# Perceiver of four layers on one core: identity products of TensorE taken out at nine places

## The reference, cut to what matters

```python
x = x + L0_xattn(ctx, ctx, _layernorm(x), ...)
x = x + L0_attn(_layernorm(x), ...)       # gated linear attention
x = x + L0_ffn(_layernorm(x), ...)        # 8 routed experts and 1 shared
x = x + L1_xattn(_layernorm(x), ctx, mask, ...)
x = x + L1_attn(_layernorm(x), ...)
x = x + L1_ffn(_layernorm(x), ...)        # 4 experts
x = x + L2_xattn(_layernorm(x), ctx, bias, ...)   # with a norm, a feed forward and a norm of its own
x = x + L2_attn(_layernorm(x), ...)
x = x + L2_ffn(_layernorm(x), ...)        # 4 rounds over 4 experts
x = x + L3_xattn(_layernorm(x), ctx, ctx, ...)
x = x + L3_attn(_layernorm(x), ...)
x = x + L3_ffn(_layernorm(x), ...)        # low rank

def _layernorm(x, axis=-1, eps=1e-05):
    m = jnp.mean(x, axis=axis, keepdims=True)
    v = jnp.var(x, axis=axis, keepdims=True)
    return (x - m) / jnp.sqrt(v + eps)
```

## The kernel before

| place | line | call | behind | ahead of | at us |
|---|---|---|---|---|---|
| 1 | L735 | (2, 2) | projection of the L0 cross attention | norm, L0 attention | 41.3 |
| 2 | L779 | (2, 2) | projection of the L0 attention | norm, gates and feed forward L0 | 80.4 |
| 3 | L791 | (2, 2) | feed forward L0 | norm, L1 cross attention | 186.8 |
| 4a, 4b | L1070 | (2, 1) | projection in `self_attention`, called for L1 and L3 | norm, feed forward L1 / L3 | 436.0, 1151.3 |
| 5 | L1176 | (2, 2) | feed forward L1 | norm, L2 cross attention | 481.1 |
| 6 | L1319 | (2, 1) | projection of the L2 cross attention | norm, its feed forward | 623.9 |
| 7 | L1322 | (2, 9) | its feed forward | two norms in a row, L2 attention | 646.2 |
| 8 | L1370 | (2, 2) | feed forward L2, four rounds | norm, L3 cross attention | 990.0 |
| 9 | L1378 | (2, 1) | projection of the L3 cross attention | norm, L3 attention | 1113.0 |

## Time and profile before

### The profile page before, as it was taken

The page is one execution under the profiler, slowest core; times in us unless marked ns, Lnnn a source line. Parts: engine busy times, 40 slices in busy tenths (PEclk is TensorE's granted clock), DMA queues, the critical chain, the costliest instruction groups (busy, mean ns, idle before and its releaser), DMA issues.

```text
span 1173.2 us, 26800 instructions
## 1 busy us (share of the span) xinstructions
PE 1087.7 (93%) x9262; PEld 752.1 (64%) x9262; DVE 678.1 (58%) x2030; ACT 581.1 (50%) x1288; POOL 347.3 (30%) x550
## 2 busy tenths in 40 slices
PE   7879998999999789899998878899999999999987
PEld 4455665787777556566665456677777776666554
DVE  5575445545555573678784775534343434788774
ACT  5542224343333464577774352634343444678665
POOL 2216101211121213355541141221304040466560
PEclk9989999999999998999999979999999999999989
DMA  8700130222232001355642412011111111100000
GB/s 264 261 1 21 33 85 8 62 48 57 57 56 62 1 2 34 122 167 160 164 132 87 102 32 47 14 54 52 57 41 55 53 55 45 50 2 2 1 2 20
DMA packets 69307, 75.32 MB, mean 64 GB/s; under 512 B 12048, under 2 KB 61472, under 8 KB 68840
## 3 DMA queue, kind: packets, MB, share of 16 engines
q1 hardware_dynamic: 67032, 66.50, 20.5%
q0 software_dynamic: 1376, 7.49, 2.0%
q10 hardware_dynamic: 816, 0.20, 0.1%
HBM read 71.55 MB, written 2.10 MB: 63 GB/s over the span
## 4 chain that ended last, share of the span: by engine, by line
PE 79%; DVE 8%; ACT 5%; DMA 3%; issue 2%; POOL 2%; ACTq 1%; SPq 0%; DVEq 0%; POOLq 0%
PE PS L566 13%; PE PS L578 12%; PE PS L1205 7%; PE PS L1216 6%; PE PS L853 5%; PE PS L817 5%; PE PS L569 3%; PE PS L860 2%; PE PS L1237 2%; PE PS L804 2%; PE PS L1194 2%; ACT XN L1446 2%; PE PS L1187 1%; PE PS L843 1%; PE PS L1232 1%
## 5 line engine op out<-in xcount | busy, mean ns | idle before, releaser
L578 PEld LDWEIGHTS PS<-WB,AR 128*128 128x128 f32 x1504 | 181.6, 192 | 42.7 <-issue 38.8
L578 PE MATMUL PS<-WB,AR 128*128 128x128 f32 x1504 | 182.3, 275 | 0.6 <-DVE X L2084 0.5
L1446 ACT ACTIVATE AR<-PS,WB 128x512 f32<-128x512 f32 x160 | 109.9, 687 | 144.7 <-PE PS L566 136.9
L2084 DVE SCALAR_TENSOR_TENSOR ACC<-PS,SM,ACC 128x128 f32<-128x128 f32 x192 | 54.1, 344 | 95.8 <-PE PS L578 94.8
L1959 DVE TENSOR_TENSOR AR<-PS,AR 128x512 f32<-128x512 f32 (+2 forms) x71 | 49.8, 701 | 92.8 <-issue 38.6
L566 PE MATMUL PS<-ZT,WB 128*128 128x512 f32 x208 | 101.1, 609 | 0.7 <-DMA WB<-in_units 0.7
L1205 PE MATMUL PS<-AR 64*128 64x257 f32 x512 | 90.6, 429 | 1.0 <-POOL AR L2929 1.0
L1446 ACT ACTIVATE AR<-PS 128x512 f32<-128x512 f32 (+2 forms) x83 | 43.8, 528 | 85.5 <-PE PS L569 69.1
L566 PE MATMUL PS<-XNT,WB 128*128 128x512 f32 x168 | 85.4, 614 | 0.4 <-DMA WB<-in_units 0.4
L1216 PE MATMUL PS<-W,AR 128*128 128x128 f32 x512 | 80.1, 282 | 1.3 <-ACT AR L1446 1.3
L2871 POOL TENSOR_TENSOR AR<-AR,SM 128x516 f32<-128x516 f32 x32 | 33.7, 1054 | 155.6 <-ACT SM L1446 93.8
(11 more groups left out here) (345 smaller groups left out, 2114.4 us busy)
## 6 DMA issues: line engine op xcount, KB each, us to landing
WB<-in_units SPq DMA_DIRECT2D x49, 385.0 KB, 3.0
CTX<-in_fside SPq DMA_DIRECT2D x32, 514.0 KB, 4.0
CTX<-in_ctxT SPq DMA_DIRECT2D x72, 130.0 KB, 2.1
CTX<-in_ctxN SPq DMA_DIRECT2D x32, 129.0 KB, 2.3
CTX<-in_ctxN SPq DMA_DIRECT2D x4, 516.0 KB, 5.8
AR<-in_ctxN SPq DMA_DIRECT2D x4, 516.0 KB, 9.6
AR<-in_ctxN SPq DMA_DIRECT2D x32, 64.5 KB, 3.1
AR<-in_l1x_w POOLq DMA_DIRECT2D x1, 2048.0 KB, 8.1
```

The source lines that it names most:

```text
L578: m = pe.matmul(PS[:, 4 + hh, 128 * t:128 * t + 128], f_h[hh][:, c, 128 * t:128 * t + 128], WB[:, q, 2 * UNIT + 128 * c:2 * UNIT + 128 * c ...
L1446: return act.activation(o, i, fn, **k)
L2084: ins = dve.scalar_tensor_tensor(out=a, in0=y, scalar=f_w[:, 4 * hh + t, bass.ds(e, 1)], in1=a, op0=ALU.mult, op1=ALU.add)
```

## The change

The nine lines go, and nothing else changes. `self_attention` is called twice, so the program loses ten stops' products: 23 matmuls of 512 columns, 46 records.

```diff
             l0_project(1)
-            keep_clock(2, 2)
...
             pe.wait_ge(sig["y_w_taken"], seen.up("y_w_taken", 4))
-            keep_clock(2, 2)
...
             ff("l0f", XNT, second=True)
-            keep_clock(2, 2)
...
                 project_half(1, w(o))
-                keep_clock(2, 1)
...
             ff("l1f", XNT, entropy, second=True)
-            keep_clock(2, 2)
...
             project(OT, w("l2x_o"))
-            keep_clock(2, 1)
             turn(Z)
             ff("l2x", ZT)
-            keep_clock(2, 9)
...
                 moe_round(r)
-            keep_clock(2, 2)
...
             project(OT, w("l3x_o"))
-            keep_clock(2, 1)
             self_attention("l3a_q", "l3a_k", 1, "l3a_o", 5, False, 10)
```

## The result

The changed kernel takes 1188.58 us (median of 20 executions, 1183.82 to 1196.95), the kernel before 1182.93 us (20 executions, 1174.04 to 1191.04). The ratio is 1.0057, 95% interval 1.0035 to 1.0079: slower by about 6.7 us; the interval leaves out both no change and a loss of 1%.

The account below looks back on a forecast made before the run. The prediction took TensorE to bound the kernel. Its terms, -0.6 + 6.3 + 0.9 + 0.9 = +7.5 us, times 0.85, were rounded to +6.5 us, put between 1181.5 and 1192.1 at 1190 us; range 1177 to 1203.

Parts of the forecast that it names:

- What bounds the kernel: Whole kernel: TensorE, busy 93% of the span, carries 79% of the chain; in nine of ten stops the norm sets readiness.
- The removed work gives back 0.6 us: Dropped products free the path almost only at place 8, 0.5 us; taken as -0.6, bounds nothing and 1 us.
- How many falls are new: 3.8, each 3.4 us: Clock falls at places 1, 3, 5, 7, 4b: 0.7 for each, 1.0 for place 7, together 6.3 us.
- The price of a fall, 1.65 us: Time lost per clock fall of 3.4 us, mean of 1.9 and 1.4 us from two pairs of equal code.
- Place 7, 2.6 us: Long gap before L2's query, key and value projections: one sure fall, plus 0.9 us for two more slow records.
- Places 2, 4a, 6, 9: nothing: Stops whose clock falls already: taken as 0, with places 6 and 9 between -1 and +1.7 us each.
- The factor 0.85: Applied to the sum of +7.5 us because DVE or ACT is sometimes the slower one behind a stop; gives 6.4.
- The base: Starting time: profiled execution 1175.0 gives 1181.5, median of timed runs 1185.6 gives 1192.1; the forecast was put at 1190.
- A: Rival: nothing to be measured, only place 7 falls; sum +1 us, 1186; chance 0.22.
- B: Rival: over 1% slower, low stretches feed themselves, 6.7 us at each of ten stops; +17 us, 1203; chance 0.23.
- C: Rival: faster, the products made the transposes late, at place 8 and perhaps 1, 3, 5; -4.5 us, 1181; chance 0.10.
- the prediction's first pair: Eight feed forward records at place 6 took 5.62 us at the low clock against 3.70; the fall cost 1.9 us.

Follow-up runs that it names:

- more products alone: Kernel before with more identity products at places 2, 4a, 4b, 6, 7, 9 and in other idle stretches: 1180.35 us, ratio 0.998.
- the fill without the nine calls: Changed kernel with one identity transpose of 128 columns ahead of each of tiles 1 to 7 in the turns: 1183.32 us, ratio 1.0017 to before.
- the fill beside them: Kernel before with one 128-column identity transpose ahead of each of tiles 1 to 7 at the ten stops and L1's self attention: 1173.65 us, ratio 0.9927.
- the fill with more products: Kernel before with both the added identity products in idle stretches and the identity transposes ahead of tiles 1 to 7: 1169.43 us, ratio 0.9870.

## Why the prediction was right, and where not

The forecast was a loss of 6.5 us, +0.55%; the measured ratio is +0.57% (0.35 to 0.79), the time 1188.6 us for 1190. The direction and the cause hold: more of the kernel runs at the lower clock, and the first products behind the norms pay for it. That the number came out this close is in part luck, since the terms of the sum were off in opposite directions.

- *What bounds the kernel* held. TensorE kept 79% of the chain, the other engines' busy times did not move, and the transposes kept waiting for ACT. That the 13% of DVE and ACT are mostly the norms, the rows do not show.
- *The removed work gives back 0.6 us.* At place 8 it gave 2.0 us at the first transpose and 1.2 at the projection, twice the term and outside its bound of 1 us. In nine stops it gave nothing that reached the next stage, as said.
- *How many falls are new: 3.8, each 3.4 us.* This term was mis-sized. All five stops that were at 1.00 fell, and of the five that fell already places 6 and 9 doubled their low time. Over the ten stretches of 14 us the low time grows from 24 to 57 us, and the kernels' means differ by as much, 110 - 76 = 34 us. The forecast was 0.008 of mean clock, 19 us; the fall is 0.014, from 0.968 to 0.954.
- *The price of a fall, 1.65 us.* Per fall it held roughly: 2.4 us at place 1, 1.4 at place 3, 1.9 at place 5, 1.1 at place 7, 0.8 at place 4b, in the mean 1.5. Per us of low clock it did not: the sum had 0.49, and it was 0.35 at place 1 and 0.28 at place 5, where the stretches were 6.8 us long, and 0.41 at place 3, where it was 3.4. Over all it is 6.7 / 34 = 0.20. At place 7 5.5 us of the low stretch of some 10 lie over the wait; at place 8 the slower projection is offset by the 1.2 us won. How the 34 us divide among these is read from one profile and not measured.
- *Place 7, 2.6 us* by the sum. In the profile 1.1 us; with only that line out 2.0 us in the profile and 4 us in the median, of which the interval leaves 0.5 to 8. Not settled.
- *Places 2, 4a, 6, 9: nothing.* -0.1, 0.0, 0.6 and 1.0 us: right for the two that stand ahead of gates, a little too low for the others.
- *The factor 0.85* for what other engines swallow was a guess from the 79%. The stops' 10 us in the profiles against 6.7 in the medians would be a factor of 0.67; no run isolates it.
- *The base.* The sum was made on an execution of before with a clock of 0.976, near the top of the 0.959 to 0.977 that 89 executions show. That a typical one has 20 us more of low time could not be seen from one profile; three times that lay 11 us apart hinted at it, and putting the forecast under 1192.1 for that reason was right.

Of the rivals, A (no fall but at place 7) is refuted by the ten stretches. B (low stretches that feed themselves) came nearer than the forecast in the clock and failed in the price. The prediction named as its sign 6.7 us and more at most of the stops, and six of ten show it; it gave 43 us more of low time beside the long gap, where 34 came in all. But B priced these at 17 us, and 6.7 was measured. Long low stretches inside a stage exist as well: 13.7 us in L1's self attention in the changed kernel, 17 us in two other executions; since the kernel before has them in some executions too, they do not count for the change. C (the products were in the way) is true at place 8 and in the middle of self attention, where moving them won 0.5%; it did not decide.

The Trainium skill, page "TensorE: Matmul & The Clock Gate", section "Terms", has half of the low time as its price. The averages here lie under it: 0.38 us per us between executions of one program, 0.20 between the two programs. A single fall onto dense products can reach it, as the 1.9 us for 3.4 of the prediction's first pair.

## What to carry to other kernels

Read TensorE's granted clock stage by stage and over several executions before pricing anything in its gaps; one profile can lie 20 us of low clock off the mean. A product that computes nothing is worth its place where TensorE waits for a norm and dense work follows, and costs most of its time as soon as it stands behind the wait instead of ahead of it (1.4 of 1.98 us in self attention). Fill both parts of such a gap, the idle one and the one in which single transposes trickle: more products alone left 51 us of low clock, the fill without the nine calls 93, the fill beside them 57, the fill with more products 38.

## What the runs showed of the hardware

- A stretch of L1's self attention, mostly products on 32 x 32 and 128 x 32 tiles, stayed at the lower level for 13 us with TensorE busy all the time (423 to 436 us of the changed kernel). Two profiles of one program, the kernel before, differ in the same way: 1.00 in the first, 0.62 over 18 us in the second. 64 records took 1.96 us at the one level and 1.14 at the other.
- With products of 8 columns in place of those of 512 the clock by slices was, but for single tenths, that of the kernel with neither, though TensorE was busy for 12.65 of 14 us at place 7.
- One program's executions lie 14 us apart (1175.6 to 1189.8 in one group of 25), and the low time goes with nearly all of it (correlation 0.94).
